# A masked attention kernel where every second tile also turns block 4 by DMA instead of on TensorE

## The reference

```python
h = jnp.maximum(_layernorm(x, axis=-1), 0.0)
scores = jnp.einsum('nd,md->nm', h, ks)
scores = jax.nn.leaky_relu(scores, negative_slope=0.2)
scores = jnp.where(adj > 0, scores, -9e15)
attn = jax.nn.softmax(scores, axis=1)
return x + jnp.einsum('nm,md->nd', attn, ks)
```

## Time and profile before

| what | value |
|---|---|
| median of 3 runs | 1599.86 us (1594.65 to 1601.03) |
| the profiled execution's own time | 1600.33 us |
| its span | 1598.5 us |
| TensorE, matmuls busy | 1563.9 us (98%) |
| VectorE busy | 1421.2 us (89%) |
| ScalarE busy | 1344.5 us (84%) |
| GpSimd busy | 1335.2 us (84%) |
| DMA transposes of exponentials | 572 |
| loads of `adj` | 512, of 512 KB each |

### The profile page before, as it was taken

How to read it: one execution, slowest core, us unless ns; L and a number is a source line. 1 busy time by engine, 2 the same in 40 slices (tenths; PEclk the granted TensorE clock), 3 DMA queues, 4 the chain that set the end, 5 groups by cost and what they waited for, 6 DMA issues and landing times.

```text
span 1598.5 us, 37557 instructions
## 1 busy us (share of the span) xinstructions
PE 1563.9 (98%) x13202; PEld 1156.3 (72%) x13202; DVE 1421.2 (89%) x2532; ACT 1344.5 (84%) x2002; POOL 1335.2 (84%) x1350
## 2 busy tenths in 40 slices
PE   5799999999999999999999999999999999999998
PEld 3477777777777777777777777777777777777777
DVE  6899888988889898998998998998899899899897
ACT  7688888888888888888888888888888888888885
POOL 3788888888888888888888888888888888888885
PEclk9999999999999999999999999999999999999999
DMA  8999999999999999999999999999999999999995
GB/s 282 283 273 271 277 270 273 294 261 280 278 278 273 274 280 290 287 265 293 287 270 289 268 289 279 273 271 285 282 258 308 274 272 291 270 276 279 266 281 102
DMA packets 700602, 437.67 MB, mean 274 GB/s; under 512 B 629760, under 2 KB 629760, under 8 KB 700416
## 3 DMA queue, kind: packets, MB, share of 16 engines
q1 hardware_dynamic: 700416, 435.27, 112.5%
HBM read 276.82 MB, written 4.19 MB: 176 GB/s over the span
## 4 chain that ended last, share of the span: by engine, by line
PE 86%; DMA 4%; ACT 3%; DVE 2%; POOL 2%; issue 2%; SPq 0%; DVEq 0%; POOLq 0%; ACTq 0%
PE ps_out L428 25%; PE ps_out L429 13%; PE ps_scores L401 12%; PE ps_scores L403 12%; PE ps_scores L402 12%; PE ps_T L412 11%; DMA keys_in<-keys_in 4%; ACT scores L501 1%; DVE scores L621 1%; POOL keys_in L337 1%; DVE mask L603 1%; POOL keys_in L339 1%; ACT scores L480 1%; ACT scores L492 1%; PE ps_out L379 0%
## 5 line engine op out<-in xcount | busy, mean ns | idle before, releaser
L339 POOL TENSOR_TENSOR keys_in<-scores,keys_in 128x512 f16<-128x512 f32 x572 | 719.2, 1257 | 46.2
L621 DVE CUSTOM_DVE_ANT_0 scores<-ps_scores,mask,minus_scale 128x1024 f32<-128x1024 f32 x512 | 654.0, 1277 | 16.8 <-PE ps_scores L403 2.2
L492 ACT ACTIVATE scores<-scores 128x1024 f32<-128x1024 f32 x512 | 537.6, 1050 | 77.6 <-DVE pair_min L621 77.6
L337 POOL CAST keys_in<-scores 128x512 f16<-128x512 f32 x572 | 460.2, 804 | 159.3 <-ACT scores L501 155.2
L501 ACT ACTIVATE scores<-scores,neg_max 128x1024 f32<-128x1024 f32 x512 | 583.1, 1139 | 0.1
L428 PE MATMUL ps_out<-keys,keys_in 128*128 128x256 f16 x2225 | 428.7, 273 | 5.2 <-DMA keys_in<-keys_in 4.8
L636 DVE TENSOR_TENSOR probsT_lo<-ps_T,probsT_hi 128x512 f16<-128x512 f32 x452 | 311.2, 689 | 125.1 <-ACT probsT_hi L509 116.6
L401 PE MATMUL ps_scores<-keysT_hi,hT_hi 128*128 128x512 f16 x1024 | 389.0, 380 | 13.6 <-DVE keysT_lo L592 8.4
L429 PE MATMUL ps_out<-keys,keys_in 128*128 128x128 f16 x2225 | 398.0, 219 | 0.0
L509 ACT ACTIVATE probsT_hi<-ps_T 128x512 f16<-128x512 f32 x441 | 260.7, 591 | 153.9 <-PE ps_T L412 150.1
L402 PE MATMUL ps_scores<-keysT_lo,hT_hi 128*128 128x512 f16 x1024 | 389.1, 380 | 0.0
(11 more groups left out here) (57 smaller groups left out, 845.5 us busy)
## 6 DMA issues: line engine op xcount, KB each, us to landing
adj_in<-in_adj_dram SPq DMA_DIRECT2D x512, 512.0 KB, 5.3
keys_in<-keys_in SPq DMA_TRANSPOSE x572, 5.5
x_in<-in_x_dram SPq DMA_DIRECT2D x16, 256.0 KB, 4.4
keys_in<-in_L_gnn_ks_dram SPq DMA_DIRECT2D x8, 512.0 KB, 7.2
out_dram<-out_tile SPq DMA_DIRECT2D x16, 256.0 KB, 3.8
keys<-keysT_hi SPq DMA_TRANSPOSE x8, 5.3
keys<-keysT_lo SPq DMA_TRANSPOSE x8, 4.8
```

The lines of the kernel that those rows point to most:

```text
L337: nc.gpsimd.tensor_copy(half[:, 0:BLOCK], probs(t, b)).then_inc(half_hi_ready, 1)
L339: nc.gpsimd.tensor_tensor(half[:, BLOCK:2 * BLOCK], probs(t, b), half[:, 0:BLOCK], ALU.subtract) \
L492: nc.scalar.activation(s, s, ACT.Prelu, alpha=1.0 / SLOPE).then_inc(leaky_ready, 1)
L621: nc.vector.tensor_tensor_reduce(out=score_pair(q, p), in0=ps_scores[:, slots, :].rearrange("p s k -> p (s k)"), in1=mask[:, (p // 2) % 2, ...
```

## The change

One list is added, with block 4 beside the nine blocks, and tiles with an odd number (but for the last, 63) take it. That is 31 tiles: 1, 3, ..., 61.

```diff
@@ -42,6 +42,7 @@
     BY_DMA = tuple(b for b in range(BLOCKS) if b % 2 == 1 or b in (12,))
     BY_PE = tuple(b for b in range(BLOCKS) if b not in BY_DMA)
+    MORE_BY_DMA = tuple(sorted(BY_DMA + (4,)))
     LAST_BY_DMA = (1, 3, 5, 7, 9)
@@ -181,7 +182,7 @@
         def by_dma(t):
-            return LAST_BY_DMA if t == TILES - 1 else BY_DMA
+            return LAST_BY_DMA if t == TILES - 1 else MORE_BY_DMA if t % 2 == 1 else BY_DMA
```

## The result

The changed kernel takes 1649.87 us (median of 6 runs, 1643.27 to 1653.99), against 1599.5 us for the kernel before in the same comparison. The ratio is 1.0311, with a 95% interval from 1.0293 to 1.0329. The profiled execution took 1651.28 us, with a span of 1649.5 us. A program's executions can fall in a slower state; two of the four of experiment 4 did, and are left out of its time.

What follows compares the result with a forecast made beforehand. The SP queue with its DMAs was taken to end last, behind TensorE's pace: 1600.3 + 52.7 (31 added transposes at 1.7 us) = 1653 us, with TensorE's saving not subtracted. The range was 1612 to 1680 us.

Steps and rivals of the forecast that it cites:

- the price: SP queue: each of the 31 added transposes costs 1.7 us, 52.7 us in all.
- two bounds: SP queue, cost of an added transpose: 1.30 us (shortest issue plus gap) to 2.17 us (mean place in a saturated tile).
- second server: SP queue with its DMAs: about 24.1 to 24.8 us a tile when it never rests, no faster than TensorE.
- the gap of 1.41 us: SP queue, later stretch, before one transpose: mostly the same waiting at another place, so little spare time.
- rival A: SP queue absorbs the added transpose in spare gaps; TensorE keeps the pace, faster: 1587 us, chance 0.11.
- B: SP queue cost partly hidden: the first third pays 20 us, later odd tiles gain 8 us; 1612 us, chance 0.12.
- TensorE's 0.43 us: TensorE, four transposes fewer in each of 31 blocks: 13.3 us saved, but turned into waiting and not subtracted.
- cover of 4.7 us: Block 7's transpose: 10.3 us from issue to first use on TensorE, less 5.6 us landing, hides the added split's 1.9 us.
- Rival C: GpSimd: block 4's split, not its DMA, delays TensorE up to 1.9 us per odd tile; 1646 us, chance 0.07.
- The pair: SP queue, blocks 12 and 13: 5.15 us for two transposes, from which some 2.75 us for the added one.
- D: SP queue: the added transpose costs the pair's full 2.75 us each time; 1686 us, chance 0.08.
- The profile's signs: Expected in the trace: waits throughout, no SP gaps, late issues, TensorE's busy time falling, GpSimd's idle time growing.

Runs made afterwards that it cites:

- experiment 4: The changed kernel with the step loop's loads of adj issued from ScalarE's queue instead of SP's: 2172.16 and 2183.44 us.
- experiment 2: The kernel before plus one unused full-size DMA transpose ahead of block 5's in the 31 odd tiles: 1659.07 us, ratio 1.0349.
- experiment 3: The changed kernel with half the data in each load of adj behind the first eight: 1581.62 us, ratio 0.9869.
- experiment 9: The kernel before plus an unused plain 256 KB copy on the SP queue in the 31 odd tiles: 1602.77 us, ratio 1.0031.
- experiment 6: The kernel before plus an unused 128 x 128 DMA transpose in the 31 odd tiles: 1598.79 us, ratio 1.0008.
- experiment 10: The kernel before plus an unused 128 x 512 DMA transpose in the 31 odd tiles: 1602.63 us, ratio 1.0027.
- experiment 12: The kernel before without block 12 by DMA, so eight blocks by DMA everywhere: 1620.94 us, ratio 1.0148.
- experiment 1: The kernel before plus GpSimd's split of block 4 into an unread buffer in the 31 odd tiles: 1605.26 us, ratio 1.0025.
- experiment 5: The kernel before with half the data in each load of adj behind the first eight: 1593.0 us, ratio 0.9966.
- 7: The kernel before with four 1 MB loads of adj for each tile in place of eight of 512 KB: 1691.46 us, ratio 1.0576.

## Why the prediction was right

The bound and the sign were right for the reason given. The size was right in part by luck: the price was a middle of two bounds, of which the lower one doesn't hold, and its error and the two terms that were left out mostly cancel.

**The bound.** That the SP queue is a second server with no room was the step on which all rests, and for a further full-size transpose it held: the earlier trace rows were the normal state to come. Experiments 2, 3 and 9 show that it is the transposes with what is in flight beside them. The reading that the gap of 1.41 us in the later stretch was not spare time also held, since the changed kernel pays in all of its run. But the gaps were no small matter: 54.9 us of them lie between 660 and 1500 us before, some 3 us for two tiles, which is more than the 1.7 us that rival A asked for. Experiments 6, 9 and 10 did use them, for little or nothing; a full transpose could not pay with them alone. Rivals A and B fall.

**The price of a transpose.** 1.7 us was taken as the middle of 1.30 and 2.17. Measured alone it is 1.86 us (experiment 2). The middle was right, its reason less so. The lower bound says that the queue can't issue anything for free, 1.30 us at least. But 31 further issues of 1.2 us and half of the data cost 5 us in all (experiment 10), 0.17 us each, and 31 of an eighth cost 0.04. And the 1.86 us are no place in the queue but what is left of some 3.5 us of issues when the gaps are used up. A mean price also suggests that each transpose costs the same, and experiments 6, 10 and 12 show a threshold. At eight blocks the median issue is 1.24 us and the queue has room (gaps of 425 us from 100 to 1500 us); the ninth makes it 1.67 to 1.82.

**TensorE's 0.43 us.** I said that it turns into waiting and isn't subtracted. The terms, added as if all counted, are 57.8 (experiment 2) + 3.9 (experiment 1) - 11.4, 13.3 or 15.5 (experiments 3 and 5) = 46.2 to 50.3 us, against 50.4 measured between the medians. That speaks for TensorE's saving still counting, and so does its busy time, 14.9 us less than in experiment 2 beside nearly the same wait. If so, this step of the prediction was wrong. But the interval of experiment 2 alone is 12 us wide, so it is likely and not shown. The forecast of 52.7 us came close with two terms missing that have opposite signs, 3.9 and some -13 us, and a price 5 us too small.

**GpSimd.** The split costs about 4 us, which I had at nothing. It would fit a cover of 4.7 us behind landing that was used up in part, but no run separates this. Rival C was right in kind, and some twelve times too large.

**The pair.** D, 2.75 us for each, is out: 1686 us against 1649.9. Its reading of the pair was not wrong, as the two pairs of one tile take 5.12 and 4.44 us; it would fit that a part of this comes out of gaps, but no run separates it.

**The profile's signs.** Two tiles in 50.0 us in the mean (49 to 50.5 forecast throughout, 48.1 to 52.1 seen), no gaps of size, issues 2 us or more behind their splits, the second x2 row above 4 us, waits in all of the run: seen. Two signs did not come. TensorE's busy time didn't fall (1564.1 against 1563.9 us), which fits the 15 us that late transposes add to it in experiment 2. GpSimd's idle time behind ScalarE hardly grew (158.6 us in all, 155.2 before), as the new splits, 47.6 us more of busy time, took what the longer run gave.

## What to carry to other kernels

Before work is moved from a busy engine to a DMA queue, read the queue as a server of its own: whether its issues follow one another without a gap, how far they stand behind the data that they wait for, and whether their median is above the shortest one. When it is near this state, one more full-size transfer can cost several times the engine time that it saves (here 1.86 against 0.43 us), even if nobody waits for it. But the length of an issue is not its price: a copy of the same bytes and a transpose of half of them passed nearly for free, so try the very transfer, alone and at its full size. And do not take the splits in a chain's list for a cause before each issue is put beside its own. The balance between two resources is a corner and not a valley: here a block too few by DMA costs 0.37 us and one too many 1.6.

## What the runs showed of the hardware

- The price of a further DMA transpose on one queue is not proportional: 128 x 128, 128 x 512 and 128 x 1024 fp16 numbers cost 1, 5 and 58 us for 31 of them, and a plain copy of the largest size 5 us. All four land after 5.5 to 5.7 us (median), whatever their size.
- The issue of a transpose is 1.24 us when landing takes 3.5 us (experiments 3 and 5) or 4.6 (12), 1.8 us when it takes 5.5, and 2.2 us when it takes 6.2 (7). It fits a queue that takes only a few transposes, some two of full size, before the oldest has landed. Counted in the trace of the changed kernel from 100 to 1500 us: when an issue begins, one or two earlier transposes are still on their way and never three (437 of 531 times two), and when it ends it is one in 509 of 531 cases. In experiment 10, where smaller ones stand between, it is two in 51 cases, and in experiment 4, with no loads in the same queue, in 200 of 376, so the loads seem to take a share of the room. The number was not tested by itself.
- With the loads on ScalarE's queue and the transposes on SP's, the same transfers took 1.32 times as long in all (the changed kernel's 1649.9 us), and transposes landed after 8.3 us (median) and up to 24.1 us.
